# A row sort in front of a mixture-of-experts stage: row numbers and weights in one round of tables, or in two

## The reference, cut to what matters

```python
x = hidden_states.reshape(T, H)                       # T = 2048, H = 512
logits = jnp.einsum('th,eh->te', x, gate_w)           # 8 experts
probs = jax.nn.softmax(logits, axis=-1)
topw, sel = jax.lax.top_k(probs, 2)
topw = topw / jnp.sum(topw, axis=-1, keepdims=True)
combine = jnp.zeros((T, E)).at[jnp.arange(T)[:, None], sel].add(topw)
gate_up = jnp.einsum('th,eoh->eto', x, w1)
g, u = jnp.split(gate_up, 2, axis=-1)
act = jax.nn.silu(g) * u                              # 352 columns
expert_out = jnp.einsum('eti,ehi->eth', act, w2)
out = jnp.einsum('eth,te->th', expert_out, combine)
```

## Time and profile before

| | |
|---|---|
| runs of the kernel | 1645.63 us median of 3 (1645.42 to 1649.64) |
| profiled execution | span 1645.2 us from the first instruction to the last; nothing around it is recorded |
| mean granted TensorE clock | 0.959 of 2.4 GHz |
| first sort and its expert stage | 433.7 to about 732 us, first gathered rows transposed at 455.7 |
| second sort and its expert stage | 1340.2 to 1645.2 us, first gathered rows transposed at 1361.6 |
| PE busy | 1513.7 us (92%), x11983 |
| PEld busy | 1273.2 us (77%) |
| DVE busy | 920.9 us (56%) |
| ACT busy | 720.4 us (44%) |
| POOL busy | 599.6 us (36%) |

### The profile page before, as it was taken

How to read it: one execution, slowest core, us unless ns; L and a number is a source line. 1 busy time by engine, 2 the same in 40 slices (tenths; PEclk the granted TensorE clock), 3 DMA queues, 4 the chain that set the end, 5 groups by cost and what they waited for, 6 DMA issues and landing times. The chain is left out here.

```text
span 1645.2 us, 34129 instructions
## 1 busy us (share of the span) xinstructions
PE 1513.7 (92%) x11983; PEld 1273.2 (77%) x12004; DVE 920.9 (56%) x2133; ACT 720.4 (44%) x1784; POOL 599.6 (36%) x473
## 2 busy tenths in 40 slices
PE   6999999998799999988799999999999879999997
PEld 5788788787588888976577787777877558888896
DVE  5677767766622234225687786867878662222221
ACT  3666666666022234325455455554545302222222
POOL 5656456455233334421233222332222303333342
PEclk9999999999799999999799999999999969999999
DMA  5355456444579786532001101010100037787753
GB/s 213 113 190 198 148 183 210 144 170 174 189 261 311 194 277 187 90 58 85 14 21 33 39 34 33 20 34 27 46 21 21 27 135 246 215 254 216 186 91 56
DMA packets 95917, 212.36 MB, mean 129 GB/s; under 512 B 7216, under 2 KB 7216, under 8 KB 94512
## 3 DMA queue, kind: packets, MB, share of 16 engines
q1 hardware_dynamic: 76736, 166.58, 28.8%
q0 software_dynamic: 17472, 40.90, 12.6%
q10 hardware_dynamic: 1584, 3.15, 0.5%
HBM read 136.94 MB, written 73.66 MB: 128 GB/s over the span
## 5 line engine op out<-in xcount | busy, mean ns | idle before, releaser
L1298 PE MATMUL bank<-ring,halves 128*128 x1872 | 331.9, 326 | 3.6 <-ACT halves L1137 3.6
L1298 PEld LDWEIGHTS bank<-ring,halves 128*128 128x128 f32 x1872 | 302.6, 188 | 10.7 <-issue 4.5
L498 POOL TENSOR_TENSOR arena<-arena 128x1024 f32<-128x1024 f32 x64 | 123.8, 1934 | 142.1 <-DVE arena L578 140.5
L1696 DVE SCALAR_TENSOR_TENSOR arena<-arena 128x256 f32<-128x256 f32 x240 | 128.4, 577 | 17.8 <-ACT arena L1915 15.0
L1592 POOL TENSOR_TENSOR arena<-arena 128x1024 f32<-128x1024 f32 x16 | 31.3, 1959 | 291.7 <-ACT arena L1969 253.4
L710 ACT ACTIVATE arena<-arena 128x256 f32<-128x256 f32 x256 | 126.3, 500 | 0.2 <-DVE arena L570 0.2
L791 PE MATMUL bank<-arena 128*128 128x128 f32 x1024 | 124.2, 280 | 1.8 <-ACT arena L691 0.8
L1147 ACT ACTIVATE arena<-bank 128x512 f32<-128x512 f32 x78 | 46.6, 598 | 180.1 <-PE bank L1329 91.5
L791 PEld LDWEIGHTS bank<-arena 128*128 128x128 f32 x1024 | 118.3, 194 | 7.7 <-issue 3.6
L1109 POOL DMA_INDIRECT arena<-normalised_rows,arena x78 | 80.4, 1031 | 101.1 <-PE bank L1281 50.1
L1117 POOL DMA_INDIRECT out_dram<-arena x39 | 61.8, 1584 | 149.0 <-issue 88.6
(11 more groups left out here) (285 smaller groups left out, 3306.9 us busy)
## 6 DMA issues: line engine op xcount, KB each, us to landing
ring<-expert_halves SPq DMA_DIRECT2D x16, 4352.0 KB, 18.9
expert_halves<-expert_high SPq DMA_DIRECT2D x16, 1088.0 KB, 8.6
expert_halves<-expert_rest SPq DMA_DIRECT2D x16, 1088.0 KB, 10.8
arena<-in_w_dram SPq DMA_DIRECT2D x8, 1088.0 KB, 6.5
normalised_rows<-arena SPq DMA_DIRECT2D x33, 256.0 KB, 2.0
arena<-in_x_dram SPq DMA_DIRECT2D x32, 256.0 KB, 2.8
arena<-mid_rows SPq DMA_DIRECT2D x32, 256.0 KB, 2.8
w_in_raw<-in_in_w_dram SPq DMA_DIRECT2D x16, 290.0 KB, 7.1
```

Of the source, the lines that this page charges most:

```text
L498: nc.gpsimd.tensor_tensor(held, held, spread(rinv[:, HG * g:HG * g + HG], 2, 2 * P), ALU.mult)\
L1298: last = nc.tensor.matmul(bank[1 + 2 * par + part][:, 0:INTER], rows_parts[a][:, par, k * P:k * P + P], weights(at, b, (2 * k + part) * IN ...
L1696: last = nc.vector.scalar_tensor_tensor(out=slot[:, j], in0=cin[:, c, k:k + PAIR], scalar=taps[:, c, k:k + 1], in1=slot[:, j], op0=ALU.mul ...
```

## The change

Both sorts change alike, since they share the code. The first round of tables holds the row numbers alone: each part is the comparison and one table operation, and `lists` multiplies one group of 40 columns a product. The weights' rounding and rest move behind the index. The two `turn` operations that need only the owner move ahead of the wait for the lists. Behind the index and the slots' numbers VectorE makes a second round of tables: eight operations, each of which compares the row-number table with 0.5 and multiplies by the weights or their rests, so that `one_hot` isn't needed again. TensorE gets a second call of `lists` with 32 products of 80 columns into bank 5, behind the register loads and ahead of `turn(0)`. The fillers behind the first lists are 9 and no longer 18. Two semaphores are added.

```diff
--- before.py
+++ after.py
@@ -1069,8 +1069,9 @@
     chain = sem("sort_chain")
     both_ready, ranks_made, gap_ready, exp_ready = sem("both"), sem("ranks"), sem("gap"), sem("exp")
     tables_ready, lists_made = sem("tables"), sem("lists")
+    w_tables_ready, w_lists_made = sem("w_tables"), sem("w_lists")
     index_ready, slots_ready = sem("index"), sem("slots")
-    rank_bank, list_bank = bank[3], bank[7]
+    rank_bank, list_bank, w_bank = bank[3], bank[7], bank[5]
     PART = TOPK * TILES // 4
     *gathered, added = core.pool_dma[tag]
     rows_turned, rows_high, rows_rest = sem("rows_turned"), sem("rows_high"), sem("rows_rest")
@@ -1222,8 +1223,6 @@
                                              spread(sort.start, 1, K * T), ALU.mult))
                 link(nc.vector.tensor_reduce(sort.place, sort.picked.rearrange("p k t e -> p (k t) e"), AX.X, ALU.add))
                 link(nc.vector.tensor_tensor(sort.place, sort.place, sort.full.rearrange("p k t -> p (k t)"), ALU.add))
-                link(nc.vector.tensor_copy(sort.w_parts, sort.w[:, 0:K]))
-                link(nc.vector.tensor_tensor(sort.w[:, K:2 * K], sort.w[:, 0:K], sort.w_parts, ALU.subtract))
                 for j in range(0, K * T, PART):
                     part, of_tile = slice(j, j + PART), slice(j % T, j % T + PART)
                     if j == PART:
@@ -1235,27 +1234,35 @@
                     link(nc.vector.tensor_tensor(one_hot, spread(sort.slot_at, 1, PART),
                                                  spread(sort.place[:, part], 2, SLOTS + 1), ALU.is_equal))
                     nc.vector.tensor_tensor(sort.by_slot[:, part, 0], one_hot, spread(core.rowid[:, of_tile], 2, SLOTS + 1),
-                                            ALU.mult)
-                    nc.vector.tensor_tensor(sort.by_slot[:, part, 1], one_hot,
-                                            spread(sort.w_parts[:, j // T, of_tile], 2, SLOTS + 1), ALU.mult)
-                    nc.vector.tensor_tensor(sort.by_slot[:, part, 2], one_hot,
-                                            spread(sort.w[:, K + j // T, of_tile], 2, SLOTS + 1), ALU.mult)\
-                        .then_inc(tables_ready, 1)
+                                            ALU.mult).then_inc(tables_ready, 1)
                 link(nc.vector.tensor_tensor(sort.past, spread(sort.slot_at[:, 0:SLOTS], 2, E - 1),
                                              spread(sort.end[:, 0:E - 1], 1, SLOTS), ALU.is_ge))
                 link(nc.vector.tensor_reduce(sort.owner, sort.past, AX.X, ALU.add))
+                link(nc.vector.tensor_scalar(sort.turn, sort.owner, float(RING), -float(RING), ALU.is_ge, ALU.mult))
+                link(nc.vector.tensor_tensor(sort.turn, sort.turn, sort.owner, ALU.add))
                 dve.wait_ge(lists_made, 1)
                 link(nc.vector.tensor_scalar(sort.empty, list_bank[:, 0:SLOTS], 0.5, core.spareid[:], ALU.is_lt, ALU.mult))
                 nc.vector.scalar_tensor_tensor(out=index, in0=sort.empty, scalar=-1.0, in1=list_bank[:, 0:SLOTS],
                                                op0=ALU.add, op1=ALU.add).then_inc(index_ready, 1)
-                link(nc.vector.tensor_scalar(sort.turn, sort.owner, float(RING), -float(RING), ALU.is_ge, ALU.mult))
-                link(nc.vector.tensor_tensor(sort.turn, sort.turn, sort.owner, ALU.add))
                 link(nc.vector.tensor_scalar(sort.again, sort.turn, float(RING), -float(RING), ALU.is_ge, ALU.mult))
                 nc.vector.tensor_tensor(place, sort.turn, sort.again, ALU.add).then_inc(slots_ready, 1)
                 nc.vector.tensor_scalar(needed, sort.owner, 16.0, 16.0, ALU.mult, ALU.add).then_inc(slots_ready, 1)
                 nc.vector.tensor_scalar(ends, sort.end, 1.0 / P, 1.0, ALU.mult, ALU.max).then_inc(slots_ready, 1)
-                link(nc.vector.tensor_copy(weight, list_bank[:, SLOTS + 1:2 * SLOTS + 1]))
-                link(nc.vector.tensor_tensor(weight, weight, list_bank[:, 2 * SLOTS + 2:3 * SLOTS + 2], ALU.add))
+                link(nc.vector.tensor_copy(sort.w_parts, sort.w[:, 0:K]))
+                link(nc.vector.tensor_tensor(sort.w[:, K:2 * K], sort.w[:, 0:K], sort.w_parts, ALU.subtract))
+                dve.wait_ge(tables_ready, 4)
+                for j in range(0, K * T, PART):
+                    part, of_tile = slice(j, j + PART), slice(j % T, j % T + PART)
+                    here = sort.by_slot[:, part, 0].bitcast(F32)
+                    nc.vector.scalar_tensor_tensor(out=sort.by_slot[:, part, 1], in0=here, scalar=0.5,
+                                                   in1=spread(sort.w_parts[:, j // T, of_tile].bitcast(F32), 2, SLOTS + 1),
+                                                   op0=ALU.is_gt, op1=ALU.mult)
+                    nc.vector.scalar_tensor_tensor(out=sort.by_slot[:, part, 2], in0=here, scalar=0.5,
+                                                   in1=spread(sort.w[:, K + j // T, of_tile], 2, SLOTS + 1),
+                                                   op0=ALU.is_gt, op1=ALU.mult).then_inc(w_tables_ready, 1)
+                dve.wait_ge(w_lists_made, 1)
+                link(nc.vector.tensor_copy(weight, w_bank[:, 0:SLOTS]))
+                link(nc.vector.tensor_tensor(weight, weight, w_bank[:, SLOTS + 1:2 * SLOTS + 1], ALU.add))
 
             sort_rows()
             nc.vector.memset(bank[5][:], 0.0).then_inc(cleared, 1)
@@ -1346,21 +1353,21 @@
                 nc.tensor.matmul(rank_bank[:, 2 * E:3 * E], core.onesb[:], sort.both[:, N + 1], start=False, stop=True)\
                     .then_inc(ranks_made, 1)
 
-            def lists():
+            def lists(out, columns, tables, done):
                 n = TOPK * TILES
                 for j in range(n):
                     if j % PART == 0:
-                        pe.wait_ge(tables_ready, j // PART + 1)
-                    last = nc.tensor.matmul(list_bank[:, 0:3 * (SLOTS + 1)], sort.at_spot[:, j // TILES, j % TILES],
-                                            sort.by_slot[:, j].rearrange("p c s -> p (c s)"),
+                        pe.wait_ge(tables, j // PART + 1)
+                    last = nc.tensor.matmul(out, sort.at_spot[:, j // TILES, j % TILES],
+                                            sort.by_slot[:, j, columns].rearrange("p c s -> p (c s)"),
                                             start=(j == 0), stop=(j == n - 1))
-                last.then_inc(lists_made, 1)
+                last.then_inc(done, 1)
 
             stay_busy(core, bank[6], 3)
             rank_last()
             stay_busy(core, bank[6], 16)
-            lists()
-            stay_busy(core, bank[6], 18)
+            lists(list_bank[:, 0:SLOTS + 1], slice(0, 1), tables_ready, lists_made)
+            stay_busy(core, bank[6], 9)
             places, needs = {}, {}
 
             def look_up(s, j):
@@ -1373,6 +1380,7 @@
             for s in range(2):
                 for j in range(2):
                     look_up(s, j)
+            lists(w_bank[:, 0:2 * (SLOTS + 1)], slice(1, 3), w_tables_ready, w_lists_made)
             turn(0)
             pe.wait_ge(weights_in, needs[0])
             up(0, 0, places[0])
```

## The result

| | before | after |
|---|---|---|
| time, median of 20 runs each | 1648.53 us (1641.08 to 1653.9) | 1653.24 us (1648.79 to 1661.55) |
| ratio after/before, 95% interval | | 1.0029 (1.0017 to 1.0041) |
| profiled execution: span | 1645.2 us | 1657.0 us |
| mean granted clock | 0.959 | 0.958 |

The changed kernel is slower by about 4.8 us (2.8 to 6.8); the forecast was 3.3 us faster. A ratio of 1.0029 lies at the edge of the 0.3% that the prediction called the limit, but the interval lies wholly above 1.

A forecast was written before the change was run, and what follows sets the result against it. Bound: the expert stage's products and accumulating transfers, with the sort on the path. Per sort 4.3 gained less 1.9 and 0.75 leaves 1.65, twice 3.3; 1645.2 becomes 1641.9, plus 0.4 gives 1642.3 us (range 1637.0 to 1648.0).

The forecast's parts named there:

- Part 1: Both sorts, up to the index: fewer table operations ahead of it bring the index 4.3 us earlier (3.4 to 4.6).
- Part 2: Between index and first gathered rows: the second round costs 0.6 to 1.0 us at high clock, about 4.0 at low.
- Part 3: TensorE's clock after fewer fillers: up products may start at 1.2 GHz, losing 0.9 to 2.1 us; 0.75 taken per sort.
- signs that the prediction named for being wrong: 40-column products well under 0.11 us, combined operations over 0.6, gather later than second round, rest of stage not shifted alike.
- Rival B: Sorts: clock falls in or right behind the nine fillers, slowing lists and up products; 4.8 us slower, 1650.4; chance 0.10.
- Rival A: Sorts: clock holds through the second round and up products; 7.0 us faster, 1638.6; chance 0.25.
- Rival C: Expert stage: starts earlier but doesn't end earlier, accumulating transfers dominating; 0 to 2 us either way, 1645.6; chance 0.10.

The follow-up runs named there:

- r6: Kernel before with 9 fillers instead of 18 behind its lists, nothing else: 1653.06 us, ratio 1.002 (1.0 to 1.0039).
- r7: Changed kernel with the second sort's weights replaced by a constant 0.5, without its second tables and lists: 1653.35 us (one run).
- r2: Changed kernel with TensorE's register loads moved: slot 0's behind its transposes, slot 1's behind the up products: 1645.11 us, ratio 0.999.
- r1: Changed kernel again, no edit: 1653.38 us (12 runs), ratio 1.003 (1.0012 to 1.0047).
- r10: Changed kernel a third time, no edit, for its profile: 1650.4 us (one run), profiled span 1648.7 us.
- r9: As r3, with 12 fillers instead of 9 behind the first lists: 1640.95 us, ratio 0.9951 (0.9935 to 0.9968).
- r3: As r2, with the last quarter of the weight lists also moved behind slot 0's transposes: 1644.26 us, ratio 0.997.
- r5: Changed kernel with 12 fillers instead of 9, and 4 more between slot 0's transposes and up products: 1648.05 us, ratio 0.9991.

## Why the prediction was wrong, point by point

**Part 1 held.** Index earlier by 4.4 on the average of three profiles (4.2 to 4.6), 4.3 said (3.4 to 4.6). Eight products of 40 columns take 0.97 at 2.4 GHz like those of 120 in the earlier trace rows: the weight loads set the pace.

```profile
443.49 0.97 PEld L1361 LDWEIGHTS bank<-att_by_slot,att_at_spot 128*128 128x128 f32 x8 [0.53 <-DVE att_by_slot L1236]
```

The turn operations and the gather moved past SP's load cost nothing, as said: the gather of the second sort went out at 1361.10, 1.08 behind the index (1.08 before too).

**Part 2 failed, and with it the forecast.** The failing step is the sentence that the register loads "come ahead of its new wait for the weight tables, and what is queued behind that wait is counted in part 2". They were seen and costed at nothing. Four loads are 2.75 us from `slots_ready` on, the first table is there 2.0 behind the index, as predicted (2.1), but the lists start 3.2 to 3.5 behind it in all six sorts of three profiles. The sentence looked only at what the new wait holds up, and not at what holds up the wait. The trace of before had their price, in the sequencer's rows, which the prediction didn't read because they were hidden there. VectorE's own terms were right or a little dear: operations 0.40 to 0.41 apart, 0.45 taken, and the last table 4.3 to 4.4 behind the index, 4.9 taken. First transposes were forecast 5.8 to 9.0 behind the index; in the three profiles of the changed kernel they are 7.4 to 10.3, mean 8.5, against 5.4 in two of before: 3.2 a sort where 1.9 was taken.

**Part 3 had the mechanism and half of its size.** Up products took 5.5 to 6.8, mean 5.9, instead of 4.11, in all six sorts of three profiles and not in half of them: 1.8, and 0.75 was taken. The 6.77 of the first sort also lies past the dearest case that it allowed, 6.2. A term was missing: the four transposes and the copy behind them, in which the kernel before needs 1.5 and the changed one, at the low clock, 2.0. The Trainium skill's rule (a gap on TensorE brings the half rate back, "TensorE: Matmul & The Clock Gate", HAM oscillation — how this bites in real kernels), which the prediction weighed and then halved, was the better guide: r6 and r7, whose only gaps are waits for the gather, have up products at 6.42, 5.66 and 6.41. Nor was it enough to say that nine fillers fewer "end before the first weight table": r6 shows that they had a second use. A good part of this miss hangs on part 2's: with the register loads out of the way, r2 has up products at 4.11 and 5.51, 0.7 lost in the mean, which is what part 3 had taken. Of the signs that the prediction named for being wrong, three didn't appear, and the fourth (the rest of the stage not shifted as its beginning) can't be told from what the slot loops vary by chance; second lists that start later than the first table weren't among them.

Put together for one sort: -4.4 for the index, +3.2, +0.5, +1.8, in all 1.1 slower, 2.2 for both (sorts' ends 57.5 against 55.3 in the mean). Forecast was 3.3 faster: 5.5 of the difference of 8.1 lies in these terms, and the rest is open (below).

**Rival B** was the right one in kind (2.4 a sort slower, given 0.10): the clock fell behind the nine fillers or in them. Its 4.8 in all is also what the medians show, but the sorts of three profiles hold only 2.2 of it; r1 comes nearest to the case it drew, 4.1 for both sorts together. Two things in it were off. The index stayed 4.4 earlier and not 3.7. And what it had in its favour was a filler block that starts cold, but in the second sorts of r1 and r10 the fillers ran at 2.4 GHz, and the clock fell all the same in the lists behind 1.75 us of idle time, a wait that it didn't foresee. **Rival A** (7.0 faster) is what r9 reaches, with another order. **Rival C** isn't borne out: what r2, r3 and r9 won at the sorts' ends against the changed kernel (7.1, 8.5, 10.9, by its mean of 57.5) they won in the median (8.3, 9.1, 12.4, against r1's 1653.38).

**What stays open.** The changed kernel is 4.8 (2.8 to 6.8) slower and the sorts account for 2.2. Over three profiles of the changed kernel and two of before, the rest of the mean span (1652.6 against 1648.1) is 1.0 at the start of the attention stage, 0.8 in the slot loops, 0.5 between the stages; the loops of the kernel before differ by 5.8 us between its two profiles, so none of these is shown to belong to the change. The same holds of r6, whose 3.9 us of median are 2.3 to 3.2 by its sorts.

## What to carry to other kernels

When a wait for another engine is put into a queue, the instructions right ahead of it in that queue are on the path from then on, register loads of the sequencer among them: price them from their own rows, even where they are hidden now. Filler products beside a wait are paid work if what follows the wait is a dense block: a cut of fillers has to be costed at the block behind, and so has each gap that a new order leaves on TensorE. When an order gives up in the middle what it has won at the start, try the same parts in another order before the idea is dropped: the change as made costs 4.8 us, in the order of r9 and with three fillers more it brings 7.8.

## What the runs showed of the hardware that wasn't expected

A lookup of a value by TensorE's sequencer (a read of 0.30 to 0.49 us, a calculation of about 0.15) costs 0.6 to 0.9 us from one load's start to the next in the profile after, and the four come one behind the other: 2.75 us.

The start of the attention stage comes in two kinds, whichever kernel it is. VectorE (L645) and GpSimd (L480) make the rests of two weight matrices at nearly the same time. In the kernel before, VectorE begins first:

```profile
21.09 3.09 DVE L645 TENSOR_TENSOR wv_rest<-arena,wv_high 128x2048 fp32r<-128x2048 f32 x1 [12.80 <-ACT wv_high L762]
...
22.12 6.48 POOL L480 TENSOR_TENSOR wo_rest<-arena,wo_high 128x2048 fp32r<-128x2048 f32 x1
```

In the profile after, GpSimd does, by 0.04 us:

```profile
22.44 4.49 POOL L480 TENSOR_TENSOR wo_rest<-arena,wo_high 128x2048 fp32r<-128x2048 f32 x1
22.48 6.60 DVE L645 TENSOR_TENSOR wv_rest<-arena,wv_high 128x2048 fp32r<-128x2048 f32 x1 [13.29 <-ACT wv_high L762]
```

In r10, the same program as the one above, the order is the other way round by 0.13 us:

```profile
22.19 2.29 DVE L645 TENSOR_TENSOR wv_rest<-arena,wv_high 128x2048 fp32r<-128x2048 f32 x1 [14.17 <-ACT wv_high L762]
...
22.32 6.58 POOL L480 TENSOR_TENSOR wo_rest<-arena,wo_high 128x2048 fp32r<-128x2048 f32 x1
```

Whichever begins second ends behind the first by nearly the time that it takes when it begins first (GpSimd 4.49, VectorE 2.29): GpSimd 4.42 behind VectorE's end in the first pair (24.18 to 28.60) and in the third (24.48 to 28.90), VectorE 2.15 behind GpSimd's in the second (26.93 to 29.08). Over all twelve profiles VectorE's result is there at 24.1 to 24.5 or at 28.5 to 29.1, and the expert stage began at 431.4 to 433.8 in the profiles of the first kind and at 435.6 to 436.4 in those of the second. The Trainium skill ("SBUF — State Buffer", SBUF: two separate sides) has the one that starts first hold a shared pair of ports for its whole instruction, and the durations agree. The expectation of r10 tied the kind to a late rise of TensorE's clock. The granted clock isn't resolved there (1.00 over all of 8 to 17 us), but the first 32 products (L791) show TensorE's pace: they took 6.34 us in r10, longer than in two profiles of the slow kind (6.20 in r1, 6.12 in r5) and than the 5.34 of the kernel before, and yet VectorE began first. So that rule doesn't hold; who starts first decides, and what decides that is open. The two kinds differ by 2 to 5 us at the start of the expert stage. That is part of the spread of 13 us between runs of one kernel, and no property of the change: the changed program shows both.
